# First layer of a graph network on one Trainium2 core: edge products with the filter index on the partitions, edge tiles streamed at 384 columns, squared edge values fetched by DMA

## The reference, cut to what matters

```python
offsets = jnp.linspace(0.0, CUTOFF, NG)                 # NG = 64
g = jnp.exp(coeff * (e[:, :, :, None] - offsets) ** 2)  # e = adj
h = ssp(einsum('bijg,fg->bijf', g, W1) + b1)            # ssp = softplus - ln 2
Wf = einsum('bijf,gf->bijg', h, W2) + b2
rf = einsum('bjd,fd->bjf', x, Wa)
y = einsum('bjf,bijf->bif', rf, Wf * A * A)             # A = adj
y = einsum('bid,ed->bie', ssp(einsum('bif,df->bid', y, Wd1) + bd1), Wd2) + bd2
```

## Time and profile before

| what | us |
|---|---|
| median of 3 runs | 1770.27 |
| profiled execution, its own time | 1770.88 |
| its span, first to last instruction | 1768.7 |
| TensorE busy | 1375.5 (78%) |
| TensorE weight loads busy | 1125.1 (64%) |
| VectorE busy | 1176.1 (66%) |
| ScalarE busy | 807.2 (46%) |
| GpSimd busy | 741.7 (42%) |
| first layer | up to about 918 |
| layers two and three | about 929 to 1250 |
| LSTM and the last layer | from about 1250 on |

### The profile page before, as it was taken

One profiled execution on the slowest core, in us unless ns is written; L12 is line 12 of the kernel. 1 busy time (PEld: TensorE's weight loads), 2 busy tenths in 40 slices (PEclk: granted clock), 3 DMA queues, 4 the chain that ended last, 5 costly groups with the idle time before them and its releaser, 6 DMA issues. The chain is left out here.

```text
span 1768.7 us, 37607 instructions
## 1 busy us (share of the span) xinstructions
PE 1375.5 (78%) x8705; PEld 1125.1 (64%) x8736; DVE 1176.1 (66%) x5246; ACT 807.2 (46%) x1921; POOL 741.7 (42%) x1378
## 2 busy tenths in 40 slices
PE   4888888888888888888854756666666788888884
PEld 3777777777777777777743545455455565555563
DVE  5777777777777777777624888888887333333337
ACT  2656565656555655556521223222232233333347
POOL 4455445544554445544533655656655100000007
PEclk9999999999999999999975688787788899999989
DMA  3332233323332333223300000000000000000003
GB/s 88 85 82 75 74 77 87 76 71 80 81 80 74 75 85 81 71 76 82 77 3 19 25 13 24 21 14 24 12 30 13 1 1 0 0 0 0 0 0 96
DMA packets 140443, 82.82 MB, mean 47 GB/s; under 512 B 64963, under 2 KB 136031, under 8 KB 140385
## 3 DMA queue, kind: packets, MB, share of 16 engines
q1 hardware_dynamic: 138660, 81.06, 17.6%
q10 hardware_dynamic: 1725, 1.13, 0.2%
HBM read 77.31 MB, written 4.82 MB: 46 GB/s over the span
## 5 line engine op out<-in xcount | busy, mean ns | idle before, releaser
L715 PEld LDWEIGHTS wf<-w2t,hid 128*128 128x128 f32 x1536 | 351.4, 315 | 36.0 <-issue 36.0
L715 PE MATMUL wf<-w2t,hid 128*128 128x128 f32 x1536 | 371.7, 396 | 0.0
L904 DVE SCALAR_TENSOR_TENSOR msg<-wf,val_sq,rfe 128x128 f32<-128x128 f32 x768 | 210.3, 343 | 177.4 <-PE wf L715 145.5
L604 ACT ACTIVATE rfe<-rg 128x768 f32<-128x768 f32 x128 | 102.7, 803 | 210.6 <-PE rg L731 210.6
L510 POOL TENSOR_TENSOR xb<-xin,bd2bc 128x128 f32<-128x128 f32 x64 | 29.2, 457 | 397.3 <-DVE xres L894 397.0
L731 PE MATMUL rg<-rf_hi,pick 128*128 128x128 bf16 x768 | 155.5, 237 | 10.3 <-issue 9.1
L731 PE MATMUL rg<-rf_mid,pick 128*128 128x128 bf16 x768 | 155.2, 237 | 0.0
L731 PE MATMUL rg<-rf_lo,pick 128*128 128x128 bf16 x768 | 154.0, 235 | 0.0
L1634 POOL MEMSET r_minus_half<- 128x4 f32 x1 | 0.1, 102 | 328.0 <-POOLq L1504 328.0
L1530 PEld LDWEIGHTS r_zgi<-xin,w_hh 128*128 128x128 f32 x508 | 67.0, 192 | 98.6 <-issue 87.7
L1582 DVE SCALAR_TENSOR_TENSOR r_new<-r_gates 128x64 f32<-128x64 f32 x128 | 28.8, 225 | 148.2 <-ACT r_gates L1563 148.2
(11 more groups left out here) (282 smaller groups left out, 3696.9 us busy)
## 6 DMA issues: line engine op xcount, KB each, us to landing
val_bc<-edge_val SPq DMA_DIRECT2D x256, 96.0 KB, 2.7
idx_bc<-edge_idx SPq DMA_DIRECT2D x128, 192.0 KB, 3.0
adj_w<-in_adj_rows SPq DMA_DIRECT2D x64, 64.0 KB, 2.4
xt_w<-in_x_cols SPq DMA_DIRECT2D x64, 64.0 KB, 2.0
adjt_w<-in_adj_t SPq DMA_DIRECT2D x64, 64.0 KB, 1.9
xin<-in_x_rows SPq DMA_DIRECT2D x32, 128.0 KB, 2.1
m_adj_g<-in_adj_rows SPq DMA_DIRECT2D x16, 256.0 KB, 2.8
m_adjt_g<-in_adj_t SPq DMA_DIRECT2D x16, 256.0 KB, 2.8
```

The costliest lines, as they stand in the source:

```text
L604: act.activation(rfe[:, q, :].rearrange("p (a n) -> p a n", a=2), rg[:, :, 0:HALF], ACT.Copy).then_inc(s["rfe_ready"], 1)
L715: last = pe.matmul(column(wf, r), h[:, r, :], w2t[:, :], start=True, stop=True)
L904: last = dve.scalar_tensor_tensor(msg[:, q, r * P:(r + 1) * P], column(wf, r), val_sq[:, q4, r:r + 1], rfe[:, q, r * P:(r + 1) * P], ALU.m ...
```

## The change

The products of the first layer are turned round, so that the filter index is on the partitions and the edge slots are columns. w2t and the three parts of the features become the loaded operands, and hid and pick are streamed, 384 columns a product. The message is then one instruction over 768 columns (wf plus b2, times rv), where rv is the gathered feature times the squared edge value. The squares come by a third store (edge_sq) and as a broadcast load of 128 x 768 float32, sq_bc (384 KB), in the place of val_own. rv is made by GpSimd (from rfe) in even units and by VectorE (straight from PSUM) in odd ones. The sums over slots are taken at a stride of six by GpSimd and gathered in y; the overflow slot is brought in behind Wd1 (over_u). adj_t, rfb, val_sq, yt and t_u are gone from this layer. b2 becomes a column. The cast of the indices (ei16), which was on VectorE, is an activation on ScalarE, and the check for negative values (least) too. found has two buffers.

```diff
 SP, load_unit and the stores
-                after(sp, "valsq_ready", u, d - UNIT_BUFS, u0)
+                after_parity(sp, "rv_even" if (u.inner + d) % 2 == 0 else "rv_odd", u, d - UNIT_BUFS)
-                sp.dma_start(val_own[:, q, :],
-                             val_src[bass.ds(gi, 1), kk, :, :].rearrange("a i r -> (a i) r")).then_inc(unit_in[q], 16)
+                sp.dma_start(sq_bc[:, q, :], sq_src[bass.ds(gi, 1), kk, :, :].rearrange("a i r -> a (i r)")
+                             .broadcast_to((P, UNIT))).then_inc(unit_in[q], 16)
-                        if g.has(1):
-                            after(sp, "adjtsq_ready", g, -1, g0)
-                            alone(sp)
-                            sp.dma_start(adjt_w[:, g.mod(2, 1), :], a["adj_t"][:, g.at(1), :])\
-                                .then_inc(adjt_in[g.mod(2, 1)], 16)
                         w(sp, "edges16", g.at(2) + 1)
+                        w(sp, "squares_ready", g.at(2) + 1)
+                        for dst, src in ((edge_val, found[:, q, 0:2 * R]), (edge_sq, squares[:, q, :]),
+                                         (edge_idx, ei16[:, q, :])):
+                            sp.dma_start(dst[bass.ds(g.at(2), 1), :, :, :].rearrange("a h i r -> (a i) h r"),
+                                         src.rearrange("p (h r) -> p h r", h=2)).then_inc(edges_stored, 16)
+                        sp.wait_ge(edges_stored, 48 * (g.at(2) + 1))
 GpSimd, body
+                        w(pool, "picks_ready", g.at(2) + 1)
+                        pool.tensor_copy(last_rank[:, bass.ds(g.at(2), 1)], found[:, q, RANKS - 1:RANKS])
+                        pool.tensor_tensor(squares[:, q, :], found[:, q, 0:2 * R], found[:, q, 0:2 * R], ALU.mult)\
+                            .then_inc(s["squares_ready"], 1)
+                        pool.tensor_tensor(rv[:, 0, :], rfe[:, :], sq_bc[:, q, :], ALU.mult).then_inc(s["rv_even"], 1)
+                        m = msg[:, q, :].rearrange("p (i r) -> p r i", r=R)
+                        pool.tensor_tensor(sum1[:, 0:wide, :], m[:, 0:wide, :], m[:, wide:2 * wide, :], ALU.add)\
+                            .then_inc(s["sum1_ready"], 1)
 ScalarE, body, at its end (t_ex and t_lg move ahead of dist2, yt is gone, rfe only if i % 2 == 0)
+                    if not dense and k_in == 0 and g.has(-1):
+                        w(act, "over_u_p", g.at(-1) + 1)
+                        act.activation(over_u[:, :], p_over_u, ACT.Copy).then_inc(s["over_u_ready"], 1)
                         act.activation(rf32[:, :], p_rf, ACT.Copy)
                         act.activation(rf_hi[:, g.mod(2, 1), :], p_rf, ACT.Copy).then_inc(s["rfhi_ready"], 1)
+                    if not dense and k_in == 0 and g.has(2):
+                        w(act, "picks_ready", g.at(2) + 1)
+                        act.activation(ei16[:, q, :], found[:, q, RANKS:RANKS + 2 * R], ACT.Copy)\
+                            .then_inc(s["edges16"], 1)
+                    if not dense and k_in == 0 and g.has(3):
+                        act.activation(minus[:, :], adj_w[:, q, :], ACT.Relu, scale=-1.0,
+                                       accum_out=least[:, bass.ds(g.at(3), 1)]).then_inc(s["least_ready"], 1)
 TensorE, body
-                        h = hid[:, q, :].rearrange("p (i r) -> p r i", r=R)
-                        for r in range(R):
-                            last = pe.matmul(column(wf, r), h[:, r, :], w2t[:, :], start=True, stop=True)
+                        for half in range(2):
+                            last = pe.matmul(wf[:, half, 0:HALF], w2t[:, :], hid[:, q, half * HALF:(half + 1) * HALF],
+                                             start=True, stop=True)
+                        for half in range(2):
+                            picked = pick[:, u.mod(2, 1), half * HALF:(half + 1) * HALF]
+                            for part in (rf_hi, rf_mid, rf_lo):
+                                last = pe.matmul(rg[:, half, 0:HALF], part[:, gn.mod(2), :], picked,
+                                                 start=part is rf_hi, stop=part is rf_lo)
 VectorE, body
-                        for r in range(R):
-                            last = dve.scalar_tensor_tensor(
-                                msg[:, q, r * P:(r + 1) * P], column(wf, r), val_sq[:, q4, r:r + 1],
-                                rfe[:, q, r * P:(r + 1) * P], ALU.mult, ALU.mult)
+                        dve.tensor_tensor(halves(rv[:, 1, :]), rg[:, :, 0:HALF], halves(sq_bc[:, u.mod(UNIT_BUFS), :]),
+                                          ALU.mult).then_inc(s["rv_odd"], 1)
+                        dve.scalar_tensor_tensor(halves(msg[:, q, :]), wf[:, :, 0:HALF], b2c[:, :],
+                                                 halves(rv[:, i % 2, :]), ALU.add, ALU.mult)\
+                            .then_inc(s["msg_ready"], 1)
```

More of the change, by code:

```diff
@@ L252, in layer0 @@
     idx_bc = sb("idx_bc", [P, UNIT_BUFS, UNIT], BF16)
-    val_own = sb("val_own", [P, UNIT_BUFS, R])
-    val_sq = sb("val_sq", [P, UNIT_BUFS, R])
+    sq_bc = sb("sq_bc", [P, UNIT_BUFS, UNIT])
     dist2 = sb("dist2", [P, HALF])
@@ L494, in body @@
+                    if dense and u.has(1):
+                        q = u.mod(UNIT_BUFS, 1)
+                        pool.wait_ge(unit_in[q], unit_count(u, 1, q))
+                        pool.tensor_tensor(sq_bc[:, q, :], sq_bc[:, q, :], sq_bc[:, q, :], ALU.mult)\
+                            .then_inc(s["valsq_ready"], 1)
+                    if i % 2 == 0 and u.has(0):
+                        q = u.mod(UNIT_BUFS)
+                        w(pool, "rfe_ready", of_parity(u) + 1)
                         if dense:
-                            pool.wait_ge(unit_in[q], unit_count(u, 1, q))
+                            w(pool, "valsq_ready", u.at() + 1)
@@ L496, in body @@
                         else:
[L497 to L501, removed]
+                            pool.wait_ge(unit_in[q], unit_count(u, 0, q))
+                        after(pool, "msg_ready", u, -2, u0)
@@ L767, in body @@
-                    if not dense and k_in == 0 and g.has(3):
-                        w(pe, "cnt", g.at(3) + 1)
-                        if g.has(1):
-                            w(pe, "rfhi_ready", g.at(1) + 1)
-                        pe.matmul(p_start, before[:, :], over_cnt[:, :], start=True, stop=True)\
-                            .then_inc(s["start_ready"], 1)
+                    if k_in == 0 and g.has(-2):
+                        w(pe, "uh_ready", g.at(-2) + g0 + 1)
+                        pe.matmul(p_out, t_h[:, :], wd2t[:, :], start=True, stop=True).then_inc(s["out_ready"], 1)
@@ L793, in rank_edges @@
                 dve.wait_ge(adj_in[q], g.pair * 16 + 16 * ((g.inner + 3) // 2 + 1))
-                if not (g.static and not g.has(2)):
-                    w(dve, "over_gathered", n - 1)
-                    w(dve, "edges16", n - 1)
+                if not g.static or g.at(3) >= 2:
+                    dve.wait_ge(edges_stored, 48 * (g.at(3) - 1))
+                if not g.static or g.at(3) >= 1:
+                    w(dve, "idxf", n - 1)
                 alone(dve)
-                adj = adj_w[:, q, :]
@@ L895, in body @@
                             .then_inc(s["res_ready"], 1)
+                    if not dense and k_in == 1 and g.has(3):
+                        place_overflow(g)
                     if u.has(0):
-                        q, q4 = u.mod(2), u.mod(UNIT_BUFS)
+                        q = u.mod(2)
                         w(dve, "wf_ready", u.at() + u0 + 1)
-                        w(dve, "rfe_ready", u.at() + u0 + 1)
-                        w(dve, "valsq_ready", u.at() + u0 + 1)
-                        after(dve, "summed", u, -2, u0)
@@ L903, in body @@
-                        for r in range(R):
-                            last = dve.scalar_tensor_tensor(
-                                msg[:, q, r * P:(r + 1) * P], column(wf, r), val_sq[:, q4, r:r + 1],
-                                rfe[:, q, r * P:(r + 1) * P], ALU.mult, ALU.mult)
-                        last.then_inc(s["msg_ready"], 1)
+                        w(dve, "rv_odd" if i % 2 else "rv_even", of_parity(u) + 1)
+                        after(dve, "sum3_ready", u, -2, u0)
+                        if not dense and k_in == 1:
+                            after(dve, "over_u_p", g, -1, 0)
```

312 lines of the change are left out of this document (145 added, 167 removed).

## The result

The changed kernel takes 2032.17 us, median of 4 runs (2027.34 to 2033.28), against 1770.37 (1770.02 to 1770.53) for the kernel before beside it: a ratio of 1.147, 95% interval 1.145 to 1.149. It is 262 us slower. The prediction had the sign and the place of the loss, and 19 of the 262 us.

A forecast was written before the change was run, and what follows sets the result against it. TensorE bounds the kernel before, at 13.66 us a graph; after the change a closed ring of stores, loads and ScalarE's cast would. Its six terms sum to 14.07 us, over 62 rounds plus the ends giving 1789 us, range 1740 to 1845.

The forecast's parts named there:

- The ring: Cast, stores, landing, loads, landing, dist2, cast, closed once a graph: 14.07 us in place of 13.66.
- SP's round: SP's own DMA-issuing round per graph, 11.3 us: the floor of any change that leaves this queue alone.
- Rival B: Faster: the ring closes nowhere and SP's 11.3 us round is the bound, 1617 us; chance 0.06.
- Terms 1, 2 and 4: Cast end to first store issued 0.24 us; first to last store issued 1.20; first to fourth load issued 1.91.
- Term 3: Last store issued to first load issued, including the stores' landing: 3.37 us, bounds 2.9 to 4.3.
- Term 5: Fourth load, sq_bc of 384 KB, from issue to landing: 3.7 us, bounds 3.0 to 4.6.
- term 6: On ScalarE, dist2 to end of hid 3.02 us, then on through the cast: 3.65 in all (3.4 to 3.9).
- The ends: First layer: first dist2 1.0 us later, at 31.3; last even dist2 to last xres about 20 us, 33.0 before.
- The clock: TensorE's granted clock, 0.95 before, should fall in the first layer, with TensorE 55% to 75% busy.
- Rival C: Slower: TensorE at half clock, with strided sum at twice its price or sq_bc at 4.6: 1847 us; chance 0.17.

The follow-up runs named there:

- e5: Kernel before, with only its last index cast (the one releasing edges16) moved from VectorE to ScalarE behind rf_hi: 1775.79 us, ratio 1.0026.
- f1: Changed kernel with the cast to ei16 ahead of dist2 and rv of even units made by VectorE from rg: 1770.83 us, ratio 0.9994.
- e1: Changed kernel with only the cast to ei16 moved ahead of dist2 on ScalarE: 1779.3 us, ratio 1.0044.
- e4: Changed kernel without the store of edge_sq, sq_bc loaded from edge_val (output differs): 1940.74 us, ratio 1.0957.
- e2: Changed kernel with sq_bc on its own semaphore, so dist2 and pick no longer wait for it: 1904.39 us, ratio 1.0755.
- e3: Changed kernel with over_u moved ahead of dist2 on ScalarE: 1922.58 us, ratio 1.0856.
- d1: c3 with a third of the selecting products (rf_lo) left out: 1751.45 us, ratio 0.9892.
- c3: Changed kernel with early cast, SP loads reordered, sq_bc's own semaphore, over_u early, squares made by ScalarE after loading, third store gone: 1739.05 us, ratio 0.9815.

## Why the prediction was wrong

**What bounds the kernel now.** The ring named there is the right object, and e5 shows how close it was to TensorE's 13.66. The 11.3 us for SP's round were read with two stores that land in 2.9 us and did not carry over to three stores and the larger loads: one turn of f1 shows 13.5 us without a wait for an engine. Rival B's 1617 did not come about even with the ring cut at the cast: e1 takes 1779.3.

**TensorE, VectorE, GpSimd, ScalarE.** wf came at 1.56 us a unit at full clock for 1.3 predicted and at 2.91 for 2.6 at half. rv on VectorE took 0.95 and the message 1.02 for 1.04 each; rv on GpSimd 1.81 for 1.9; its strided sum 1.28 for 1.01. VectorE's 9.2, GpSimd's 8.3 and ScalarE's 8.0 us a turn stand against 9.1, 8.7 and 8.1. None of it decided anything.

**Terms 1, 2 and 4** held within 0.1.

**Term 3, 3.37, measured 4.55, outside its bounds of 2.9 to 4.3.** I added the issue of a third store and let it land like the second. It landed 1.2 us later (4.1 against 2.9); e4, with two stores again, brings the term back to 3.66. The wait is for the last landing, and that price was never in the term.

**Term 5, 3.7, measured 4.96, outside 3.0 to 4.6.** I extrapolated from 96 and 192 KB, both read where nothing as large stood around them. Beside sq_bc, idx_bc itself takes 4.0 for 3.0, so the extrapolation stood on a base that moved. That the large load did this is the likely reading; no run here takes it out. e2 shows 1.9 us a turn for taking sq_bc out of what dist2 waits for.

The Trainium skill, page "DMA: Bandwidth & Descriptors", section "Anatomy of one DMA", which is on DMAs issued from GpSimd, put the 384 KB 0.45 us behind the 192 KB. The trace, of DMAs issued by SyncE, has 4.9 against 4.0, twice that, and 4.9 where the 3.0 of the earlier trace rows with the page's step gave 3.45. It does not agree, and the measurement decides.

**The hand-over in term 6 is the step that failed in kind.** The prediction reads: "rf32 waits for p_rf, which on TensorE stands behind zb, wf, over_u and rg. ... It is close, and I cost it at nothing." I asked only whether TensorE's amount of work fits into the turn. But p_rf also waits for ScalarE's over_u of the graph before, which stands behind dist2 and hid in the same queue. So TensorE cannot use the pause: each turn it waits 6.1 us for over_u, then computes p_rf, and rf32 waits for that, 1.36 us from hid to rf32 where my steps leave 0.36 at most. e3 moves over_u and takes 1.65 us off the turn. The place to ask was in the earlier trace rows, where rf<-mb already waits 1.77 us for PE mb L741; the cause was not in any row, since the kernel before has no over_u, but it stood in the changed program, where the wait for over_u_ready comes right before p_rf. (Term 6 is also added up wrongly: its steps, 3.02, 0.18, 0.18, 0.16 and 0.2, come to 3.74 and not to 3.65.)

**The ends** were off as well: the first dist2 came 6.5 us later for 1.0 predicted; the tail is 27.0 for 20. Both are small beside 63 turns of 4.07 us more.

**The clock.** It fell from 0.95 to 0.75 as forecast. It does not make the loss: e1 has 0.77 between 100 and 800 us and yet is within 0.5% of the kernel before. Of the ring's steps it touches only p_rf, 0.77 us for its two products. Rival C had the sign and half of the cause. Its long landing came (4.9 us for the 4.6 it named), but its other way to 15 us a turn was TensorE's work, which is not what filled the turn, and 2032 is above its 1847 too.

So the mechanism was right, and the sum of its terms 3.6 us a turn short: a third store's landing, a broadcast of 384 KB and its neighbours, and a wait of another engine inside ScalarE's part of the ring. The profiled execution, 2027.34 us, missed 1789 by 238. Between the first dist2 and the last even one 1110.4 us were measured for 884.3 predicted, 226 of the 238; the first dist2 (5.5) and the tail (7.0) give the rest.

## What to carry to other kernels

Before a step that releases transfers is put into an in-order queue, follow the queue upwards: if anything ahead of it waits for the transfers that it releases, every latency between them adds up once a turn, and then each instruction on that way must be asked what it waits for on every other engine, not only how much work those engines have. Put such a step ahead of the wait; in this kernel 0.21 us of work in the wrong place cost 253 us, and in the kernel before, whose ring just fitted into the turn, 5. When a bound is lifted and the turn does not move, look for a second one of the same length before giving up on the edit: the gain came only when the transfers and the rv hand-over were both eased.

## What the runs showed of the hardware

- Three stores of 3 to 6 KB issued 0.5 us apart land 2.1, 2.9 and 4.1 us after their issue; with the middle one left out (e4), the last takes 3.2. In f1, where the loads of adj_w and xt_w are issued just ahead of them, the three take 2.6, 3.5 and 4.6 (e1: 2.5, 3.3 and 4.5). Small stores are not independent of one another.
- A broadcast load of 384 KB takes 4.9 to 5.0 us, and a 192 KB load issued just before it 4.0 where it took 3.0 without such company.
- With a third of the selecting products left out (d1 against c3) TensorE was granted a clock of 0.75 in place of 0.85 and was busy for 568 us in place of 551 in the same window; the kernel took 1751 us against 1739.
- GpSimd's sum over 128x384 with a stride of six elements takes 1.28 us where the contiguous one took 1.01. VectorE's over_t, 128x128, takes 0.86 us in the changed kernel for 0.30 before. In all 59 turns of 100 to 1150 us GpSimd's strided sum of 128x256 is under way when it starts, and it ends 0.08 us after that sum. How long it takes follows what is left of GpSimd's instruction at its start: 0.29 us with 0.1 left or less (55 of 59 turns of the kernel before), 0.31 with 0.23 and 0.75 with 0.67 (two turns each there), 0.49 with 0.41 (57 of 59 turns of e5), 0.87 with 0.78 here. Its rows in the groups of the changed kernel and of the kernel before:

```profile
L918 DVE TENSOR_SCALAR over_t<-iota_row,over_row 128x128 f32<-128x128 f32 x64 | 54.9, 859 | 0.0
```

```profile
L879 DVE TENSOR_SCALAR over_t<-iota_row,over_row 128x128 f32<-128x128 f32 x64 | 19.3, 302 | 3.3
```

The Trainium skill, page "SBUF — State Buffer", section "SBUF: two separate sides", says that VectorE and GpSimd share one pair of ports, which a VectorE instruction in a two-port mode and a GpSimd instruction lock against each other for their whole length. The ends of over_t, 0.08 us behind the sum wherever more than 0.2 us of it was left, agree with it. Whether over_t runs in such a mode no row shows.
